# Layer 1 rebuilt: VectorE passes over two key tiles, maxima by halves of the queries, rows through transfers

## The reference

```
Wh = x @ W                                   # per batch, 2048 x 256
s_i = Wh @ a1 ; s_j = Wh @ a2
e = leaky_relu(s_i[:, None] + s_j[None, :], 0.2)
e = where(adj > 0 or i == j, e, -inf)
h_prime = softmax(e, axis=-1) @ Wh
x = layernorm(x + elu(h_prime), eps=1e-5)
```

## Time and profile before

| | |
|---|---|
| median of 3 runs | 3981.21 us (3978.74 to 4451.86) |
| the profiled execution | 3980.02 us, its span 3978.2 us |
| PE busy | 3643.7 us, 92% |
| DVE busy | 3254.2 us, 82% |
| ACT busy | 2520.5 us, 63% |
| POOL busy | 2064.1 us, 52% |

### The profile page before, as it was taken

One profiled execution on the slowest core, in us unless ns is written; L12 is line 12 of the kernel. 1 busy time (PEld: TensorE's weight loads), 2 busy tenths in 40 slices (PEclk: granted clock), 3 DMA queues, 4 the chain that ended last, 5 costly groups with the idle time before them and its releaser, 6 DMA issues. The chain is left out here.

```text
span 3978.2 us, 135900 instructions
## 1 busy us (share of the span) xinstructions
PE 3643.7 (92%) x57428; PEld 2511.2 (63%) x57428; DVE 3254.2 (82%) x3989; ACT 2520.5 (63%) x3554; POOL 2064.1 (52%) x1068
## 2 busy tenths in 40 slices
PE   6999999999999999999999999942998998999898
PEld 2656756655756655665665675522776777777777
DVE  6786887787788688688788778857989989889897
ACT  3666666666666666666666666622677676776777
POOL 1786787777678687678677768831101011011010
PEclk9999999999999999999999999976999999999999
DMA  6010010010010001001001000042111110110101
GB/s 216 3 37 16 14 40 14 19 35 19 14 40 14 14 19 40 14 14 40 18 15 35 19 14 19 19 164 78 39 43 33 44 54 24 52 54 22 33 28 37
DMA packets 106692, 145.28 MB, mean 37 GB/s; under 512 B 3792, under 2 KB 87632, under 8 KB 104016
## 3 DMA queue, kind: packets, MB, share of 16 engines
q1 hardware_dynamic: 104816, 135.80, 10.2%
q10 hardware_dynamic: 1248, 0.40, 0.1%
HBM read 102.63 MB, written 33.55 MB: 34 GB/s over the span
## 5 line engine op out<-in xcount | busy, mean ns | idle before, releaser
L277 POOL TENSOR_TENSOR psums<-probs 128x1024 f32<-128x1024 f32 x512 | 1288.8, 2517 | 626.7 <-ACT probs L381 624.4
L381 ACT ACTIVATE probs<-probs 128x1024 f32<-128x1024 f32 x1024 | 1083.5, 1058 | 812.8 <-DVE probs L857 791.2
L493 PE MATMUL ctx_ps<-probs,v_rows 64*32 64x512 f32 x16256 | 1477.1, 590 | 11.7 <-DVE seg_ctx L780 10.3
L857 DVE SCALAR_TENSOR_TENSOR probs<-sc_ps,clip_hi 128x1024 f32<-128x1024 f32 x1024 | 1225.0, 1216 | 217.6 <-PE sc_ps L480 206.6
L480 PE MATMUL sc_ps<-q_cols,k_cols 64*32 64x512 f32 x16384 | 1205.0, 592 | 43.9 <-DVE probs L857 43.3
L1324 PE MATMUL out_ps<-wh,e 128*128 128x257 f32 x4096 | 963.7, 388 | 166.0 <-DVE e L1466 157.2
L1324 PEld LDWEIGHTS out_ps<-wh,e 128*128 128x128 f32 x4096 | 777.5, 193 | 326.6 <-DVE e L1466 117.9
L493 PEld LDWEIGHTS ctx_ps<-probs,v_rows 64*32 64x32 f32 x16256 | 664.0, 106 | 289.9 <-issue 190.6
L480 PEld LDWEIGHTS sc_ps<-q_cols,k_cols 64*32 64x32 f32 x16384 | 533.8, 106 | 333.9 <-issue 212.2
L1153 POOL TENSOR_TENSOR rstd<-var_eps,minus_half 128x4 f32<-128x4 f32 x32 | 68.4, 2138 | 1069.6 <-DVE var_eps L1426 1069.6
L487 PE MATMUL den_ps<-psums,ones 64*32 64x512 f32 x4064 | 598.3, 594 | 17.9 <-DVE seg_ctx L780 11.2
(11 more groups left out here) (97 smaller groups left out, 3356.1 us busy)
## 6 DMA issues: line engine op xcount, KB each, us to landing
x_cols<-in_xT SPq DMA_DIRECT2D x8, 2048.0 KB, 7.9
probs<-in_adjT SPq DMA_DIRECT2D x16, 1024.0 KB, 8.4
x_rows<-in_x SPq DMA_DIRECT2D x32, 512.0 KB, 4.1
x<-res SPq DMA_DIRECT2D x32, 512.0 KB, 2.9
x_in<-x SPq DMA_DIRECT2D x8, 2048.0 KB, 10.3
x_res<-x SPq DMA_DIRECT2D x32, 512.0 KB, 4.7
out<-h SPq DMA_DIRECT2D x32, 512.0 KB, 3.2
e<-in_adjT SPq DMA_DIRECT2D x8, 1024.0 KB, 7.8
```

Of the source, the lines that this page charges most:

```text
L277: pool.tensor_tensor(psums[:, q % 2, pair, :], probs[:, (SJ * q) % RING, pair, :], probs[:, (SJ * q + 1) % RING, pair, :], ALU.add).then_i ...
L381: act.activation(probs[:, n % RING, pair, :], probs[:, n % RING, pair, :], ACT.Exp, scale=DH ** -0.5).then_inc(s_exp, 1)
L493: return pe.matmul(ctx_ps[quad(h), z, :], v_rows[head_rows(r), n % JB, at:at + QUAD], probs[head_rows(r), n % RING, h, :], start=start, st ...
L857: dve.scalar_tensor_tensor(out=probs[:, n % RING, pair, :], in0=sc_ps[:, p, :, :], scalar=-LIM, in1=clip_hi[:, j, c * CW:(c + 1) * CW][:, ...
```

## The change

Only `layer1` and its call in `build` change.

- VectorE's two passes of a step (`larger_sides`, `mask_two`) go over two key tiles at once, every second step, 1024 elements instead of 512. `e` becomes a ring of 16 tiles, `e_low` one of 8, and ACT is 7 steps ahead.
- The maxima are made by halves of the queries, 16 passes over 1024 for each half: the first half at steps 9 to 35 of the batch before, the second at 42 to 62 and on at steps 0 to 8 of the batch itself. POOL reduces each half on its own, into `highest`.
- s_i is now a further column of `wh` (column 0), written to DRAM and read back with 8 values on each partition (`spread_own`). The four row operations run on 128 x 8 values per half (`row_operations`, steps 51 and 15), go to DRAM, and come back on all partitions in two transfers (`make_rows`). The four products L1295 and their copies are gone.
- x comes in four pieces through two buffers, and `prepare` mixes transposes with the products of `wh`, all at steps 1 to 28.
- The mask holds 0 and -2**126 instead of +-1e38, made by one DVE instruction a piece, by halves of the queries; the ring `e` is the staging buffer of all pieces.
- ELU plus one comes from one ACT pass, exp(h - 1) of the scaled h + 1, and one DVE pass (`elu`, min 1 and max). The residual is added by four instructions that also give the sum of each row; the mean shift is taken out in ACT squares whose accumulated sums give the variance (`square_h`).
- PE ends a chunk with banks 2 and 3 first (`EARLY` = 1), and begins it with four steps of banks 0 and 1 (`LATE` = 4, before 3).

```diff
-    ERING = 8
-    AHEAD = 3
-    LRING = 4
+    ERING = 16
+    AHEAD = 7
+    LARGER_AHEAD = 2
+    LRING = 8
+    LATE = 4
+    EARLY = 1
+    INV_AT, ELU_AT, RES_AT, STATS_AT, OFFSET_AT = 2, 5, 7, 8, 10
+    SQUARE_AT = 8
+    SCALE_AT, EXP_AT, NORM_AT = 3, 3, 12
+    MAX_AT = (9, 42)
+    ROWS_AT = (51, 15)
+    FIFTHS_AT = 45
...
+            def spread_own(b):
+                sp.wait_ge(s_prepread, count(b, USES, 2 + USES))
...
+                    sp.dma_start(s_d[0].rearrange("(j p) -> p j", p=P), wh[:, b[1] % 2, :, 0]).then_inc(s_sout, 16)
...
+                sp.dma_start(s_c[:, :, :], s_d[0].rearrange("(h p j) -> p h j", h=2, p=P)).then_inc(s_sin, 16)
...
+            def make_rows(b, half, first=False):
+                sp.wait_ge(s_all, count(b, 2, 2 + half + 1))
+                sp.dma_start(m_c[:, :], highest[0:1, :].rearrange("o (q j) -> o q j", j=HJ)).then_inc(s_m, 16)
+                sp.wait_ge(s_rows, count(b, 8, 4 * half + 4))
+                sp.dma_start(rows_d[half].rearrange("r (p j) -> p r j", p=P), rows_c[:, :, :]).then_inc(s_rout, 16)
+                sp.wait_ge(s_rout, count(b, 32, 16 * half + 16))
...
+                sp.dma_start(high[:, at], rows_d[half, 0].partition_broadcast(P)).then_inc(s_rin, 16)
+                sp.dma_start(low[:, at], rows_d[half, 1].partition_broadcast(P)).then_inc(s_rin, 16)
...
             def steps(b, chunks, prev, more):        # POOL
                 for c in chunks:
+                    if c == 0:
+                        reduce(b, 1)
                     if c == NC - 1 and more:
-                        reduce(following(b))
+                        reduce(following(b), 0)
                     if prev:
                         inverse_deviation(*chunk_before(b, c))
...
-                dve.tensor_scalar(piece.bitcast(F32), piece, 0, 2 * BIG, ALU.is_gt, ALU.mult).then_inc(s_flag, 1)
...
+                dve.tensor_scalar(mask[:, 4 * q:4 * q + 4, c * CW:(c + 1) * CW],
+                                  stages[i % 4].rearrange("p (a i) -> p a i", a=4), 0, -BIG, ALU.is_le, ALU.mult)\
+                   .then_inc(s_mask, 1)
...
+                    dve.tensor_tensor_reduce(out=h[:, c % 2, t, :], in0=h[:, c % 2, t, :], in1=x_res[:, c % 2, t, :],
+                                             scale=1.0, scalar=0.0, op0=ALU.add, op1=ALU.add,
+                                             accum_out=sums[:, t:t + 1]).then_inc(s_r, 1)
...
+                    act.activation(e_h[:, t, :], h[:, c % 2, t, :], ACT.Square, bias=less_mean[:, t:t + 1],
+                                   accum_out=squares[:, t:t + 1]).then_inc(s_sq, 1)
...
+            def larger_sides(b, n):
+                tiles = e[:, n % ERING:n % ERING + 2, :]
+                dve.wait_ge(s_lo, count(b, STEPS, n + 2))
+                dve.wait_ge(s_hi, count(b, STEPS, n + 2))
+                dve.tensor_tensor(tiles, tiles, e_low[:, n % LRING:n % LRING + 2, :], ALU.max).then_inc(s_max, 2)
...
+            def mask_two(b, n):
+                c, j = divmod(n, JB)
+                tiles = e[:, n % ERING:n % ERING + 2, :]
+                dve.wait_ge(s_max, count(b, STEPS, FREE + LRING + n + 2))
+                dve.scalar_tensor_tensor(out=tiles, in0=mask[:, j:j + 2, c * CW:(c + 1) * CW], scalar=BIG,
+                                         in1=tiles, op0=ALU.add, op1=ALU.min).then_inc(s_e, 2)
```

More of the change, by code:

```diff
@@ L29 @@
 ALPHA = 0.2
-BIG = 1.0e38
+BIG = 2.0 ** 126
 CW = 512
@@ L1078, in layer1 @@
         adj_v = adjT.rearrange("(q a p) (c i) -> c q p a i", p=P, a=4, i=CW)
+        pieces = [(q, c) for h2 in range(2) for q in range(4) for c in (2 * h2, 2 * h2 + 1)]
         block = ctx.enter_context(nc.Block())
@@ L1119, in steps @@
+                    if c == NC - 1 and more:
+                        make_rows(following(b), 0)
                     if not prev:
@@ L1366, in fifths, with maximum @@
[L1366 removed]
+                dve.wait_ge(s_prepread, count(b, USES, 2 + USES))
+                dve.tensor_scalar(s_fifth[:, p, :], wh[:, p, :, 1], ALPHA, None, ALU.mult)\
                    .then_inc(s_fifths, 1)
[L1369 removed]
+            def maximum(b, half, j):
                 p = b[1] % 2
[L1371 removed]
+                own, of = best[:, half, :], mask[:, j, half * HW:(half + 1) * HW]
+                dve.wait_ge(s_prepread, count(b, USES, taken(j)))
@@ new lines, in prologue, with maximum_first @@
+                row_operations((0, 0), 0)
+                for i in range(NC * 3, NC * 4):
+                    mask_piece(i)
+                for j in range(AT_START):
+                    dve.wait_ge(s_diag, JB)
+                    dve.wait_ge(s_mask, NC * 4)
+                    maximum((0, 0), 1, j)
+                for n in range(0, LARGER_AHEAD, 2):
+                    larger_sides((0, 0), n)
+            def maximum_first(j):
+                dve.wait_ge(s_diag, min(j + 1, JB // 2))
+                dve.wait_ge(s_mask, 2 * (j // 4) + 2)
+                maximum((0, 0), 0, j)
@@ L1481, in steps @@
-                        if more:
-                            for m in range(JB):
-                                if n == max_at(m):
-                                    maximum(following(b), m)
-                            if n == max_at(JB - 1) + 1:
-                                fifths(following(b))
-                            if n in ROWS_AT:
-                                row_operation(following(b), ROWS_AT.index(n))
+                        if prev and j == STATS_AT:
+                            stats(*before)
@@ new lines, in steps @@
+                        if prev and j == OFFSET_AT:
+                            offset(*before)
+                        for due in maxima(b, n, more):
+                            maximum(*due)
+                        if n == FIFTHS_AT and more:
+                            fifths(following(b))
+                        if n == ROWS_AT[1]:
+                            row_operations(b, 1)
+                        if n == ROWS_AT[0] and more:
+                            row_operations(following(b), 0)
```

422 lines of the change are left out of this document (222 added, 200 removed).

## The result

| | before | after |
|---|---|---|
| median | 3980.07 us (3978.74 to 4451.86, 4 runs) | 3909.94 us (3901.32 to 3911.23, 4 runs) |
| profiled execution, its span | 3980.02, 3978.2 | 3909.21, 3907.5 |
| first product of layer 1 | 2760.06 | 2745.32 (predicted 2738.5) |
| from there to the end | 1218.1 | 1162.2 (predicted 1101.8) |
| PE, DVE, ACT busy | 3643.7, 3254.2, 2520.5 | 3568.7, 3098.6, 2546.7 |

The ratio is 0.982 with a 95% interval of 0.9801 to 0.984; the run of 4451.86 us is an outlier and not in it. The kernel became faster by 70 us instead of 138. It is 67.2 us more than predicted, by spans: 6.8 before the first product and 60.4 behind it.

What follows compares the result with a forecast made beforehand. DVE was taken to bound three of four chunks, PE the other. First product 2738.5, batches 130, 831 (six at 138.5) and 125.4, and 15.4 at the end gave span 3840.3, or 3843 us against the median; range 3785 to 3895.

Steps and rivals of the forecast that it cites:

- rival 2: Returning from POOL's reduction routine costs as much as entering it: power 5.8 us later in 7 batches, 3884 us; chance 0.18.
- The new wait: In c0 DVE waits for POOL's power behind the second half's reduction; PE stalls 6.7 us, 11.5 in the last batch.
- the way back: POOL's return from the reduction's routine to the power in c0, counted within a first power of 3.02 us.
- The way in: On POOL ahead of each reduction, time waiting for nothing shown: 5.6 to 6.0 us, counted as 5.8.
- the 2.4: Stall at the start of c0, since DVE arrives 4 us behind after c2 and c3: 2.4 us.
- DVE's need: DVE's work in chunks c0 to c3: 31.5, 32.6, 27.1 and 30.8 us; sum 122 a batch, before 139.
- The first product: At the prologue's end, layer 1's first product comes at 2738.5, 21.5 us earlier (bounds 12 and 28).
- rival 3: Rows land late ahead of tile 64; ACT, then DVE and PE stand: 4015 us at 42 us landing; chance 0.05, partly 0.05.
- the ring's passes: DVE's larger side and mask on 1024 elements: 72.6 us a batch, gain 4.2; sign: mean near 1.22 us.
- the sums: DVE's four sums with residual per chunk, 0.375 us each, gain 5 a batch; sign: near 0.42.
- the tail: The stretch after the last batch's chunks to the end of the kernel: 15.4 us, unchanged.
- Rival 1: The wait for POOL's power in c0 is hidden by DVE's lead: 52 us fall away, 3791 us; chance 0.18.

Runs made afterwards that it cites:

- experiment 1: On the changed kernel, POOL in c0 computes the power ahead of the second half's reduction instead of behind it: 3816.97 us, ratio 0.9589 of before.
- experiment 2: On the changed kernel, the second half's reduction is replaced by an ordinary POOL operation writing a constant: 3802.66 us.
- experiment 3: On experiment 1, one more ordinary POOL addition that nothing waits for stands right behind each reduction: 3816.24 us.
- experiment 8: On experiment 1, the prologue issues the last four adjacency pieces ahead of the first rows' transfers; row operations follow the first piece: 3806.89 us.
- experiment 9: On the changed kernel, power first, loop over batch pairs written out and last prologue pieces ahead of the first rows, all together: 3797.20 us.
- experiment 10: On experiment 9, second half's maxima spread over 36 steps instead of 32, its row operations at step 18 instead of 15: 3782.28 us, ratio 0.9501 of before.
- experiment 11: On experiment 10, the prologue issues pieces 8 to 11 earlier, and DVE fills its waits with two masks and eight second-half maxima: 3783.23 us.
- experiment 4: On the changed kernel, 24 unused products keep PE busy ahead of step 11 of c0: 3897.09 us.
- experiment 6: On experiment 1, layer 1's loop over pairs of batches is written out, so no engine branches back: 3807.50 us.

## Why the prediction was wrong

Its size was off by 67.2 us; the mechanism, c0's wait for a power behind a reduction, was named with the right place and the right waiting engines, and the idle time of 15 us ahead of `nmr` that it gave as the sign of rival 2 is what came. The runs divide the miss as follows.

- **The new wait: +35.7 us** (87.4 against 51.7). The step that failed is "the first power behind a reduction took 3.02 us, the others 1.39", used as the whole price of the way back. It is 6.8 + 1.05. The row was read although 20.92 us of idle stood ahead of it; the prediction said itself that a load could have hidden there, and gave that case 0.18 as rival 2, at 3884. Nor are 3.02 us a sign of the way back: in the kernel before, the power in c1, with no reduction between it and the power before, takes 3.17 us; 1.4 is the size in c0 and c2 alone. Experiments 1 to 3 show that rival. Chain: 18.2 instead of 12.6, DVE's stand 15.1 instead of 9.7, PE's 10.7 instead of 6.7. The way in (6.2, counted 5.8) and the reduction of half the columns (3.24, counted 3.1) were right. The Trainium skill (GPSIMD Engine Reference, Instruction dispatch) speaks of about 6 us for the first call to a freshly loaded routine; the traces agree, 5.5 to 6.5 on the way in apart from 7.6 to 8.2 in the prologues of experiments 8 to 11. On the way back they show 6.7 to 7.7 ahead of an addition or a power, and none ahead of the select (experiment 3).
- **How it adds up, in those 35.7.** On PE the batch of 144.3 closes: 131.0 of work, 10.7 of idle time in c0, 1.2 + 1.5 in c3. Forecast were 128.4, 6.7, 2.4 and 1.0 for small waits. So the 2.4 was right in size, the idle time in c0 is 4.0 longer, and PE's work 2.6 longer, of which 2.0 are gone in experiment 2 (129.0), where the clock stays high. Filling the idle time (experiment 4) gives back only 0.2 to 1.2 of a batch without a branch, where DVE stands idle for some 15 us as before. The difference to experiment 2 is 12.7 a batch, to experiment 1 only 10.8, because there the moved reduction makes the waits of 2.28 and 1.06.
- **The loop's branch: +12.4** by spans from the first product (1062.4 in experiment 6 against 1074.8), 9.5 by medians. It was not in the sum at all. In the kernel before it was part of the 155.9, and a sum that is built anew from paces loses it.
- **The rest behind the first product: +12.3.** Without the wait the sum has 1050.1 and experiment 6 takes 1062.4; 6.8 of that in the six whole batches, 132.8 to 133.3 where 131.8 were counted. Most of it comes with the reduction of the second half beside a working DVE: in experiment 2, without it, a batch takes 131.6, and all that is left of the miss behind the first product is 8.2 us, the two branches of 2.9 included. DVE's need was put at 122 and is 126.2, also because maxima run at a pace of 1.20 instead of 1.135 (3059.42 to 3060.62 above), 2.0 a batch; experiment 2's 131.6 has that need in it (126.9), so it didn't make the batch longer than forecast.
- **The first product: +6.8.** The first half's maxima end at 2693.0, not 2686. The reduction and rows then took 15.8 (2693.0 to 2708.8), as counted, and the last mask is at 2725.7 instead of 2718.

What was right: rows land some 6 to 7 us after their operations (4.3 and 5.1 us for the two broadcasts), where 12 were counted, and behind the first product ACT waits for them nowhere, so rival 3 has nothing; the ring's passes (1224 and 1216 ns) and the sums (418); the powers in the other chunks, for which DVE waits 1.1 us at most; the tail (14.9 from the last inversion, 15.4 counted). Rival 1 (3791, the wait hidden) is what experiment 1 builds, and it comes to 3817, 26 more; by spans it is 28.4, of which 3.7 lie before the first product, and 24.7 are the branch and the rest.

## What to carry to other kernels

Price a PartitionAllReduce on POOL with a gap on both sides, and read the gaps only from a row with no idle time ahead; 7 us are invisible until something waits behind them. When an engine's queue gains a long operation that waits for late data, put whatever others wait for ahead of it: here two moved lines were worth 93 us by medians (87.4 behind the first product), more than the rewrite (70). Then look at who waits for the operation that was moved back: here DVE did, 2.3 us a batch, and not any more with its reader three steps later (experiment 10). When a sum is made from paces, keep a term for what the paces leave out, branches above all.
